# Two layers of cross-attention and feed-forward on one core: probabilities turned in the tiling mode of the scores, VectorE's copy set between two maxima, one scaling for two heads

## What is computed

```
x = x + xattn0(layernorm(x), ctx)     # 16 heads of 64, softmax over 375 context rows, bias
x = x + ffn0(layernorm(x))            # 8-bit rows, ternary weights, depthwise conv of 3, silu
x = x + xattn1(layernorm(x), ctx)     # 16 heads of 16, q and k with rms norm and rope
x = x + ffn1(layernorm(x))            # relu, uint8 activations with one scale over the whole batch
```

```
attn = softmax(q @ k.T * scale)       # 112 x 375
out  = attn @ v                       # 112 x 64 or 112 x 16
```

## Time and profile before

| | |
|---|---|
| median of 3 runs | 2452.87 us (2451.51 to 2453.61) |
| profiled execution | 2455.66 us |
| its span | 2453.8 us |
| busy: TensorE / its weight loads | 2380.4 / 1796.5 us |
| busy: VectorE / ScalarE / GpSimd | 1700.6 / 1584.0 / 1596.3 us |
| mean granted TensorE clock | 0.985 |

### The profile page before, as it was taken

One profiled execution on the slowest core, in us unless ns is written; L12 is line 12 of the kernel. 1 busy time (PEld: TensorE's weight loads), 2 busy tenths in 40 slices (PEclk: granted clock), 3 DMA queues, 4 the chain that ended last, 5 costly groups with the idle time before them and its releaser, 6 DMA issues.

```text
span 2453.8 us, 59494 instructions
## 1 busy us (share of the span) xinstructions
PE 2380.4 (97%) x18926; PEld 1796.5 (73%) x18926; DVE 1700.6 (69%) x4476; ACT 1584.0 (65%) x4337; POOL 1596.3 (65%) x1862
## 2 busy tenths in 40 slices
PE   7999999999999999999999999999999999999578
PEld 5777777777777777777777777777777777777336
DVE  6666666776667667666767776666677666767775
ACT  4666666766666676666666766666676666667346
POOL 2666776666667666666776666677666666766507
PEclk9999999999999999999999999999999999999689
DMA  4100000000000000000000000000000000000202
GB/s 151 35 10 10 10 8 4 8 10 10 10 10 8 10 2 10 10 10 10 10 8 4 8 10 10 10 10 8 7 5 10 10 10 10 8 4 0 55 10 61
DMA packets 34652, 37.02 MB, mean 15 GB/s; under 512 B 2932, under 2 KB 33092, under 8 KB 34628
## 3 DMA queue, kind: packets, MB, share of 16 engines
q1 hardware_dynamic: 34628, 36.71, 5.0%
HBM read 29.36 MB, written 7.34 MB: 15 GB/s over the span
## 4 chain that ended last, share of the span: by engine, by line
PE 86%; ACT 5%; DVE 4%; issue 2%; POOL 1%; DMA 0%; ACTq 0%; POOLq 0%; DVEq 0%; SPq 0%
PE ps L334 24%; PE ps L409 15%; PE pt L419 14%; PE pa L431 5%; PE pa L466 5%; PE ps L393 5%; PE pa L446 4%; ACT prob L773 3%; PE pa L334 2%; PE pt L334 2%; PE pa L593 1%; PE pa L553 1%; DVE nmx L1008 1%; PE pt L577 1%; PE ps L459 1%
## 5 line engine op out<-in xcount | busy, mean ns | idle before, releaser
L1008 DVE TENSOR_REDUCE nmx<-ps 112x2 f32<-112x750 f32 x512 | 476.5, 936 | 203.4 <-PE ps L409 203.3
L1442 POOL TENSOR_TENSOR prob<-prob,rinv 112x375 f32<-112x375 f32 x512 | 404.0, 810 | 286.6 <-DVE rinv L1024 280.6
L1442 POOL TENSOR_TENSOR f1w_room<-f1w_room,rinv 112x375 f32<-112x375 f32 x512 | 404.6, 814 | 33.4 <-DVE rinv L1024 27.2
L734 ACT ACTIVATE room<-ps 128x375 f32<-128x375 f32 (+2 forms) x480 | 227.8, 488 | 278.3 <-PE ps L334 278.3
L999 DVE COPY probT<-pt 125x336 f32<-125x336 f32 x512 | 253.0, 494 | 98.8 <-PE pt L419 98.6
L734 ACT ACTIVATE probT<-pt 125x336 f32<-125x336 f32 x512 | 233.7, 456 | 107.8 <-PE pt L419 104.9
L419 PEld LDWEIGHTS pt<-ident,prob 112*125 112x125 f32 x1536 | 191.5, 189 | 130.3 <-issue 91.7
L419 PEld LDWEIGHTS pt<-ident,f1w_room 112*125 112x125 f32 x1536 | 197.8, 188 | 119.4 <-POOL f1w_room L1442 52.7
L1465 POOL TENSOR_TENSOR krs<-krs,nhalf 125x48 f32<-125x48 f32 x32 | 256.9, 8028 | 0.0
L419 PE MATMUL pt<-ident,f1w_room 112*125 112x112 f32 x1536 | 238.2, 287 | 2.8 <-DVE probT L999 1.2
L419 PE MATMUL pt<-ident,prob 112*125 112x112 f32 x1536 | 239.1, 291 | 0.0
(11 more groups left out here) (262 smaller groups left out, 5168.7 us busy)
## 6 DMA issues: line engine op xcount, KB each, us to landing
ctok<-in_ctx SPq DMA_DIRECT2D x32, 375.0 KB
xin<-in_x SPq DMA_DIRECT2D x32, 112.0 KB, 2.0
x_rows<-x SPq DMA_DIRECT2D x32, 112.0 KB, 1.9
out<-probT SPq DMA_DIRECT2D x16, 224.0 KB, 2.3
room<-x_rows SPq DMA_DIRECT2D x1, 2576.0 KB, 13.9
stage<-in_f1w SPq DMA_DIRECT2D x2, 1024.0 KB, 5.3
stage<-in_wk SPq DMA_DIRECT2D x1, 1024.0 KB, 8.0
stage<-in_wv SPq DMA_DIRECT2D x1, 1024.0 KB, 10.5
```

What stands on the lines that cost most here:

```text
L734: return act.activation(dst, src, ACT.Copy)
L1008: top = dve.tensor_reduce(nmx[:, g:g + 2], ps[0:T, 2 * (i % 2):2 * (i % 2) + 2, 0:S], AX_X, ALU.max, negate=True)
L1442: pool.tensor_tensor(prob(i, n), prob(i, n), rinv[:, g:g + 1].to_broadcast([T, S]), ALU.mult).then_inc(s["normed"], 1)
```

## The change

Four things are changed.

1. `turn` uses the scores' tiling: each piece of 125 columns is turned in two transposes, rows 0-63 into bank 0 and rows 64-111 into bank 1 (`ROWS`), twelve in place of six, with the copies' waits and both heads' `normed` ahead of all, and a one-column bf16 matmul on rows 0-63 as the first instruction. The layout of the banks is now head, piece, row.
2. The copies follow: ScalarE takes rows 0-63 of both heads (384 columns), VectorE rows 64-111 of both (288 columns). Both wait for the whole turn.
3. In even steps from 2 on, VectorE takes the maximum of head 0, then copies the turned pair, then takes the maximum of head 1. `turned` leaves its old place in these steps.
4. The two scalings of the maxima in layer 1 become one TENSOR_TENSOR on two columns (`max_scale`), behind the reciprocal of the pair before. It waits for the maxima by a semaphore of its own, `top1`, in place of `link`.

```diff
-DVE_STEPS = 29
+DVE_STEPS = 21
...
         AHEAD = 2
+        ROWS = ((0, 64), (64, T))
...
             def turn(i, part, b):
 
+                if part != OPENING or i >= 1:
+                    pe.wait_ge(s["pT_even"], at(i, part, b))
+                    pe.wait_ge(s["pT_odd"], at(i, part, b))
+                pe.wait_ge(s["normed"], 2 * at(i, part, b) + 2)
+                pe.matmul(pt[:, 0, 511:512], identb[0:64, :], identb[0:64, 0:1], start=True, stop=True)
                 for n in range(2):
-                    pe.wait_ge(s["normed"], 2 * at(i, part, b) + n + 1)
-                    if part != OPENING or i >= 1:
-                        pe.wait_ge(s["pT_odd" if n else "pT_even"], at(i, part, b))
                     for t in range(KT):
-                        last = pe.transpose(pt[0:SK, n, t * T:(t + 1) * T],
-                                            prob(i, n)[:, t * SK:(t + 1) * SK], ident[0:T, 0:T])
-                    last.then_inc(s["pT"], 1)
+                        for bank, (r, e) in enumerate(ROWS):
+                            col = (n * KT + t) * (e - r)
+                            last = pe.transpose(pt[0:SK, bank, col:col + e - r],
+                                                prob(i, n)[r:e, t * SK:(t + 1) * SK], ident[r:e, r:e])
+                            if n == 1 and t == KT - 1:
+                                last.then_inc(s["pT"], 1)
...
             def turned(i, part, b):
 
-                act.wait_ge(s["pT"], 2 * at(i, part, b) + 1)
-                copy(probT[:, 2 * (i % 4), :, :], pt[0:SK, 0, 0:KT * T].rearrange("p (k t) -> p k t", k=KT))\
-                    .then_inc(s["pT_even"], 1)
+                act.wait_ge(s["pT"], 2 * at(i, part, b) + 2)
+                copy(probT[:, 2 * (i % 4):2 * (i % 4) + 2, :, 0:64],
+                     pt[0:SK, 0, 0:2 * KT * 64].rearrange("p (n k t) -> p n k t", n=2, k=KT)).then_inc(s["pT_even"], 1)
...
             def turned(i, part, b):
 
                 dve.wait_ge(s["pT"], 2 * at(i, part, b) + 2)
-                dve.tensor_copy(probT[:, 2 * (i % 4) + 1, :, :],
-                                pt[0:SK, 1, 0:KT * T].rearrange("p (k t) -> p k t", k=KT))\
+                dve.tensor_copy(probT[:, 2 * (i % 4):2 * (i % 4) + 2, :, 64:T],
+                                pt[0:SK, 1, 0:2 * KT * (T - 64)].rearrange("p (n k t) -> p n k t", n=2, k=KT))\
                     .then_inc(s["pT_odd"], 1)
 
-            def row_max(i, part, b):
+            def row_max(i, part, b, heads=slice(0, 2)):
 
                 layer, p = pair_of(i, part)
-                g = layer * H + 2 * p
+                g, m = layer * H + 2 * p, 2 * (i % 2)
                 dve.wait_ge(s["scores"], at(i + 1, part, b))
-                top = dve.tensor_reduce(nmx[:, g:g + 2], ps[0:T, 2 * (i % 2):2 * (i % 2) + 2, 0:S], AX_X, ALU.max,
-                                        negate=True)
+                top = dve.tensor_reduce(nmx[:, g + heads.start:g + heads.stop],
+                                        ps[0:T, m + heads.start:m + heads.stop, 0:S], AX_X, ALU.max, negate=True)
+                if heads.stop == 2 and layer == 0:
+                    top.then_inc(s["maxed"], 1)
+                elif heads.stop == 2:
+                    top.then_inc(s["top1"], 1)
+
+            def max_scale(i, part, b):
+                layer, p = pair_of(i, part)
                 if layer == 1:
-                    link(top)
+                    g, h = H + 2 * p, HEADS1[2 * p]
+                    assert HEADS1[2 * p + 1] == h + 4
+                    dve.wait_ge(s["top1"], b * PAIRS + (p + 1))
                     if p % 2 == 0:
                         dve.wait_ge(s["q1_rstd"], b * 4 + (p // 2 + 1))
-                    for n in range(2):
-                        h = HEADS1[2 * p + n]
-                        top = dve.tensor_scalar(nmx[:, g + n:g + n + 1], nmx[:, g + n:g + n + 1], qrs[:, 2, h:h + 1],
-                                                None, ALU.mult)
-                top.then_inc(s["maxed"], 1)
+                    dve.tensor_tensor(nmx[:, g:g + 2], nmx[:, g:g + 2], qrs[:, 2, h:h + 5:4], ALU.mult)\
+                        .then_inc(s["maxed"], 1)
...
                 for i in range(count):
                     if part == OPENING and i in (2, 4, 6):
                         ternary(1, i // 2 + 1)
-                    if i + AHEAD < count:
+                    between = i >= 2 and i % 2 == 0 and i + AHEAD < count
+                    if between:
+                        row_max(i + AHEAD, part, b, slice(0, 1))
+                        turned(i - 1, part, b)
+                        row_max(i + AHEAD, part, b, slice(1, 2))
+                    elif i + AHEAD < count:
                         row_max(i + AHEAD, part, b)
                     if part == MIDDLE and i == 0:
                         query_masks(b)
                     if i + 1 < count:
                         row_sum(i + 1, part, b)
+                    if i + AHEAD < count:
+                        max_scale(i + AHEAD, part, b)
                     if part == MIDDLE and i == 0:
                         query_squares(b)
-                    if i >= 1:
+                    if i >= 1 and not between:
                         turned(i - 1, part, b)
```

More of the change, by code:

```diff
@@ L212, in xattn_ffn_kernel @@
             "x_in ctx_in cT_ready cT_hi cT_lo k0_ready k0_sb v0_ready v0_sb var0 rstd0 xn0_ready xT0_ready xT0_sb "
-            "q0_ready q0_sb xbo_ready scores maxed exped recip normed pT pT_even pT_odd pv o_sb wo_ready x1_ready "
+            "q0_ready q0_sb xbo_ready scores top1 maxed exped recip normed pT pT_even pT_odd pv o_sb wo_ready x1_ready "
             "var1 rstd1 xq_ready diag_ready xqT_ready rb_ready xqT_sb rb_sb kv1_ready kv1_sb h_ready h_sb conv0 "
@@ L1231, in rest @@
                         row_max(i, CLOSING, b)
+                        max_scale(i, CLOSING, b)
                     row_sum(0, CLOSING, b)
```

## The result

The changed kernel takes 2553.73 us (median of 4 runs, 2550.21 to 2558.76) against 2452.19 (4 runs, 2450.04 to 2453.61): a ratio of 1.0415, with a 95% interval from 1.0398 to 1.0432. It is slower by 101.5 us. Its profiled execution took 2552.04 us with a span of 2550.2, 96.4 longer than before's. The forecast was 2525 within 2420 to 2590.

What follows compares the result with a forecast made beforehand. TensorE was taken as the bound, barely, with 0.2 us of room in the even loop, which would grow to 4.44. 31 x 2.3 = 71 plus 1.5 for the closing part gave 2525 us at the median's level, range 2420 to 2590.

Steps and rivals of the forecast that it cites:

- TensorE remains the bound: Whole pass, rival: changeovers go and other waits hide; 2.5 us gained a pass, 2374, any mixture up to 2448; chance 0.17.
- The turn: Twelve transposes, loads paired side by side: 0.71 us instead of 0.84; scores behind a turn 0.63 instead of 0.82.
- faster ones: Turn's loads, rival: small transposes at 0.055 each pair, even loop 4.17, 2481 us, down to 2448; chance 0.13.
- ones after another: Turn's loads, rival: twelve intervals of 0.108 lengthen each turn by 0.65; 2725 us, or 2620 if half overlaps; chance 0.08.
- The even loop: Layer 1, even-step scores through turn, copy, second half maximum, exponentials to next scores: 4.44 and 4.55 us, against 4.15.
- Without the copy in between it would be 3.8: Loop of an even pair without VectorE's copy between the maxima: 0.84 + 1.07 + 0.33 + 1.40 + 0.14 = 3.8 us.
- They go: Turns' waits for VectorE's copy, 0.68 us a pass, were to disappear with the copy's move.
- One scaling in place of two saves 0.13: Between second half maximum and exponentials in layer 1: one scaling instruction instead of two saves 0.13 us.
- The late part of the pass: Turn(13) at 67.6 instead of 65.9, next keys' first product 68.4 instead of 66.6; 2.3 us late at the end.
- The rest of the pass runs as it does: After the two turns between products, everything moves with TensorE, so nothing is added to the 2.3 us a pass.
- the reciprocal's new place: VectorE's reciprocal ahead of the scaling: in odd steps it waits for late exponentials, and scaling, copy and next exponentials wait behind.
- the wait for both heads: Start of a turn: it needs both heads normalised, so GpSimd's second product, 0.77 us later, counts.

## Why the prediction was right, point by point

**The bound and the sign: right.** TensorE's own time stayed (2384.1 for 2380.4 us) and waits came on top. The rival "TensorE remains the bound" failed at the point that was named for it: the loop is 4.5, far over 3.6.

**The turn: right.** Scores(3) to scores(4) was to take 0.71 + 0.63 = 1.34 and takes 1.32 (before 1.65). The twelve loads of a turn take 0.74 us in all where nothing holds them up (at 1297.13 above), as the six did in 0.73; in the turn at 1295.42 they are spread over 0.80. So loads of a pair do go side by side. Both rivals on the loads, faster ones and ones after another, fall.

**The even loop: right in size and in its terms.** Forecast 4.44 and 4.55, measured 4.49 and 4.58 (scores(8), (10) and (12) in the table). The copy was to start 1.56 behind the start of streaming and does so at 1.57 (1296.43 less 1294.77 and 0.09). Copy to second half 0.35: 0.38. Half maximum to scaling 0.66: 0.66. Scaling to exponentials 0.33: 0.33. The forecast of scores(14), 24.8 behind scores(3), met 24.88. And the second half maximum does stand in this loop: 0.2 us shorter, it made the pass 0.7 shorter.

**What it was put down to: wrong by half.** "Without the copy in between it would be 3.8" looks at one loop. The kernel with the split rows alone has no copy in between and cycles of 4.52, through the banks of `pt`. The prediction had the fact, four turns a pass waited for VectorE's copy, and took it as a loss that the move cures; it didn't ask what becomes of that wait when the first transpose, not the fourth, needs the copy. "They go" is wrong even in after: its turns wait 32.7 us for VectorE's copy, 1.06 a pass, more than the 0.68 that were to go. The forecast held because in the whole change the loop that was costed is the longer one, and that was luck: the other wasn't costed. Had the change been the turn alone, these steps would have forecast a gain of up to 2.5 us a pass where the run lost 2.2.

**"One scaling in place of two saves 0.13": wrong as a rule.** In the loop above it is 0.16 us long with the exponentials 0.33 behind its start, as forecast, and 194 of after's 256 are under 170 ns. Elsewhere it waits for GpSimd, as the three kernels that change the scaling alone show: each is slower than before.

**The late part of the pass: mis-sized.** Forecast for turn(13) 29.3, measured 29.62. Its row, and VectorE ahead of it:

```profile
1311.86 0.46 DVE L1005 COPY probT<-pt 125x288 f32<-125x288 f32 x1
...
1312.56 0.17 PE L419 MATMUL pt<-identb 64*128 64x1 bf16 x1 [0.72 <-DVE probT L1005]
```

Scores(3) of that pass start at 1282.93. The copy of turn(12) ends 29.39 behind them (forecast 29.2) and the turn starts 0.24 later, where I had 0.1. Two of the prediction's small sums are off by a tenth: its own terms give a net gain of 2.6, not 2.5, for the rival, and 1.8 and two turns at 0.2 give 2.2 us at the end of a pass, not 2.3.

"The rest of the pass runs as it does" is where the other 0.3 us were lost. The last turn of a pass, before and after, with what hangs on it on ScalarE and VectorE:

```profile
1273.86 0.81 PE L419 MATMUL pt<-ident,f1w_room 112*125 112x112 f32 x6
1274.37 0.45 ACT L734 ACTIVATE probT<-pt 125x336 f32<-125x336 f32 x1 [1.64 <-PE pt L419]
...
1275.25 0.41 ACT L734 ACTIVATE v<-ps 125x256 f32<-125x256 f32 x1
1275.68 0.42 DVE L1039 TENSOR_REDUCE krs<-room 125x16 f32<-125x256 f32 x1 [0.47 <-ACT v L734]
```

```profile
1320.93 0.88 PE L424 MATMUL pt<-ident,f1w_room 48*125 48x48 f32 x12
...
1321.88 0.49 ACT L740 ACTIVATE probT<-pt 125x384 f32<-125x384 f32 x1 [2.17 <-PE pt L424]
...
1322.79 0.40 ACT L740 ACTIVATE v<-ps 125x256 f32<-125x256 f32 x1
1323.23 0.42 DVE L1051 TENSOR_REDUCE krs<-room 125x16 f32<-125x256 f32 x1 [0.89 <-ACT v L740]
```

ScalarE's copy starts 0.51 behind the turn before, after half of it, and 0.95 behind now, since it needs all twelve transposes. The copy of the values and VectorE's `krs` inherit the delay: 1.82 before, 2.30 now. VectorE's chain goes on in order to the low halves of the context (L978), and the next pass's first product for the keys, which waits for them, starts 6.44 behind that turn before and 6.76 now. That is the 0.3 by which all kernels with split rows have their scores(3) late, and it continues as a wait:

```profile
1327.69 0.30 PEld L335 LDWEIGHTS ps<-cT_hi,wk_lo 128*128 128x128 f32 x2 [0.32 <-DVE cT_lo L978]
```

**The account of the 96.4 us of span.** 30 passes at 2.77 are 83.1. The first pass is 4.4 shorter (60.1 for 64.6), the start 0.4 longer. The passes 2 to 31 have 8.7 more than the 83.1, and the part behind the last pass 8.6 more. The clock has a part in three of these. The first pass holds this stretch, before and then after (stretch; busy time and instructions of PE, PEld, DVE, ACT, POOL; granted clock, 1.00 for 2.4 GHz and 0.50 for 1.2):

```profile
44.80:55.00 10.20, 10.20 (x52) 7.19 (x54) 7.83 (x11) 5.73 (x19) 7.21 (x8) 0.50 0.00 0
```

```profile
44.80:55.00 10.20, 8.41 (x110) 6.38 (x112) 9.20 (x20) 7.28 (x24) 9.20 (x10) 1.00 0.01 2
```

Before runs 10.2 us of its first pass at half the clock, after none. The kernels with 3.4 us at half in it took 61.2, 61.4 and 63.4, the one with 6.8 took 62.0, those with 10.2 took 63.5 to 64.6, and those with 23.9 took 68.1 and 68.4. So I take the 4.4 us, by which after comes out better, for the clock's doing and not the change's; why the clock stays at half for so different times there, no run shows.

**The clock, in no step of the prediction.** Three stretches of 3.4 us of one pass of after (stretch; busy time and instructions of PE, PEld, DVE, ACT, POOL; granted clock):

```profile
1360.20:1363.60 3.40, 3.23 (x45) 2.20 (x43) 2.63 (x8) 2.51 (x9) 3.40 (x5) 1.00 0.00 0
1363.80:1367.20 3.40, 2.64 (x34) 1.98 (x32) 2.37 (x7) 2.63 (x8) 3.40 (x5) 1.00 0.00 0
1367.20:1370.60 3.40, 3.40 (x29) 2.81 (x30) 1.01 (x4) 2.73 (x9) 2.82 (x4) 0.50 0.00 0
```

TensorE is idle for 0.76 of 3.4 us, in pieces under 1 us, and then runs at half its clock, 1.2 GHz, for 3.4 us. Such a pass takes 75.2 to 75.3 in place of 73.7; after has six of them, 9 us, and that is the 8.7. Before has none in its loop, nor has the kernel with the old turn. The kernel with the reciprocal behind the scaling has twelve: its passes 2 to 31 sum to 8 us more than after's, with the same median. The kernel with the copies behind the maxima has ten and the one with the split rows alone has two; at the same median pass that is 11.7 us between them. Every kernel with split rows has such passes. The one with the old turn has none, though its TensorE waits 75.7 us in all for exponentials, copies and GpSimd. The spread of after's runs is wider (8.5 us) than before's (3.6). But idle time alone doesn't say when: at the same place of the passes that keep the clock TensorE is as idle (busy 2.64 of 3.4 us), and why only some passes fall isn't shown.

Behind the last pass the clock is at half in both kernels for a long stretch in which TensorE has little to do. The same columns, before:

```profile
2240.00:2277.00 37.00, 33.07 (x314) 23.36 (x310) 24.95 (x60) 21.66 (x64) 25.73 (x36) 1.00 0.13 29
2277.20:2324.80 47.60, 27.08 (x126) 17.13 (x128) 32.70 (x83) 18.72 (x50) 27.94 (x21) 0.50 0.20 47
```

After:

```profile
2328.00:2367.20 39.20, 33.44 (x400) 23.82 (x398) 24.16 (x59) 22.70 (x67) 25.71 (x36) 1.00 0.10 23
2367.40:2432.00 64.60, 41.73 (x296) 30.68 (x297) 38.03 (x93) 24.38 (x64) 32.71 (x27) 0.50 0.16 38
```

It falls 77.0 us behind the last pass before and 79.4 after: 2.4 later, near the 1.5 that were forecast for the closing part. But it comes back after 48 us before and only after 65 in after. The kernel with the short maximum of head 0, as slow in every other respect, has its clock back for a time after 20 us. It spends 58.5 us of this part at half the clock, after 80.5, and it needs 255.5 us for it, not 262.3: 0.31 us for each us at half. Before spends 64.1 at half, 16.4 less than after. My estimate is therefore that about 5 of the 8.6 are the clock and 3.5 the waits, for which 1.5 were forecast; this is read from two kernels, not tried by itself.

Together, forecast 72.5 of span and measured 96.4: 14.1 for 30 passes at 0.47, less 2.3 since the forecast had 31 passes and the first one isn't longer, 8.7 for the clock in the loop, 7.1 more than the 1.5 behind it, less 4.4 for the first pass, and 0.4 at the start: 23.6 of the 23.9. The other 5 of the 29 us between forecast and result are the profiled executions: after's lies 1.7 under its median, before's 2.8 over.

**Two reasons that fell.** The prediction held the reciprocal's new place and the wait for both heads responsible for delays. The first costs nothing in a pass. The second couldn't be separated from the cost of a further one-column matmul.

## What to carry to other kernels

Costing a change to one loop is half the work: list every loop that has the same resources (here the scores' banks and the turn's banks), and for each the instruction that first needs what the other engine frees. An edit that makes the first instruction of a group wait for what only the last one needed takes away the cover, though nothing gets slower. And before two small instructions are made one, look at what form it takes: a short operation with two inputs in SBUF can last until the product ends that GpSimd has running, 0.8 us here in place of 0.16.

## What the runs showed of the hardware

- A VectorE product of 112x2 elements with both inputs in SBUF takes 139 to 164 ns with GpSimd idle or at its powers of 112x4 (1.01 us each), and up to 0.87 us beside GpSimd's products of 112x375 (0.81 us each; the longest is in the kernel with the reciprocal behind the scaling). With one column, the form with a scalar operand takes 201 to 216 ns where the form with two inputs takes 144 to 784.
- Transposes on rows 0-63 and 64-111 of the array with loads of 125 columns each run side by side: twelve loads in 0.74 us, as six in 0.73 on all rows.
- TensorE's granted clock fell to half for 3.4 us in 6 passes of 31. Ahead of each fall it was busy for 2.64 of 3.4 us, with gaps each under 1 us, but in the same place of the passes that kept the full clock it was as idle. Each time cost 1.5 us.
- The first pass of the loop took 60.1 us with no time at half the clock, 64.6 with 10.2 us of it and 68.1 with 23.9.
- Behind the loop the clock stayed at half for 48 us in one kernel and for 65 in the other, though the feed-forward there is the same. Of two kernels with the same median pass, the one with 22.0 us less at half was 6.9 us quicker in this part.
